# A diffusion transformer block on eight cores: FFN weight loads wait for their own prepared tile instead of for all of them

## The reference

```python
mod = (_silu(L0_c) @ L0_wmod).reshape(8, 6, 1, -1)     # sa, ca, ga, sb, cb, gb
h = _layernorm(x) * (1 + ca) + sa
x = x + ga * local_attn(h, Wq, Wk, Wv, Wo)             # 16 heads, window 512
h = _layernorm(x) * (1 + cb) + sb
gate = silu((h @ fp8(gate_w)) * gate_scale)            # 2048 -> 6144
up   = (h @ fp8(up_w)) * up_scale                      # 2048 -> 6144
x = x + gb * ((gate * up) @ fp8(down_w)) * down_scale  # 6144 -> 2048
```

## Time and profile before

| | us |
|---|---|
| time, median of 2 runs | 4372.17 (4331.66 and 4412.68) |
| the profiled execution, its own time | 4323.63 |
| its span (slowest core, core 4) | 4322.1 |
| TensorE matmuls busy | 3254.9 (75%) |
| VectorE / ScalarE / GpSimd busy | 795.2 / 773.0 / 387.8 |

### The profile page before, as it was taken

One profiled execution on the slowest core, in us unless ns is written; L12 is line 12 of the kernel. 1 busy time (PEld: TensorE's weight loads), 2 busy tenths in 40 slices (PEclk: granted clock), 3 DMA queues, 4 the chain that ended last, 5 costly groups with the idle time before them and its releaser, 6 DMA issues.

```text
span 4322.1 us, 48357 instructions; the slowest of 8 cores (4306.8 to 4322.1 us)
## 1 busy us (share of the span) xinstructions
PE 3254.9 (75%) x16778; PEld 1534.0 (35%) x16778; DVE 795.2 (18%) x1682; ACT 773.0 (18%) x1329; POOL 387.8 (9%) x520
## 2 busy tenths in 40 slices
PE   2344559976666699400299996999969999789999
PEld 0011224444443444200144443444434444344444
DVE  3200100035555510200011013111130110311101
ACT  2100401146565522200001002100011100021100
POOL 1001000011212111222100000000100000000000
PEclk9566679998889899655699997999979999889999
DMA  8897462477777778877522232222422223312233
GB/s 175 172 152 125 70 67 25 39 69 63 61 63 61 63 80 98 102 62 61 73 77 78 88 120 95 78 74 86 124 103 69 78 74 117 130 56 78 75 113 100
DMA packets 475303, 377.73 MB, mean 87 GB/s; under 512 B 384928, under 2 KB 387680, under 8 KB 470720
## 3 DMA queue, kind: packets, MB, share of 16 engines
q0 software_dynamic: 372928, 181.67, 35.5%
q1 hardware_dynamic: 102144, 192.97, 13.9%
HBM read 505.40 MB, written 62.96 MB: 132 GB/s over the span
## 4 chain that ended last, share of the span: by engine, by line
PE 55%; DMA 30%; issue 7%; DVE 3%; another core or an unknown queue 2%; ACT 1%; POOL 0%; DVEq 0%; POOLq 0%; ACTq 0%; SPq 0%
PE PSf L857 16%; PE PSf L919 15%; PE PSf L867 15%; DMA u_scr<-pre 8%; DMA g_scr<-pre 8%; DMA d_scr<-pre 7%; DMA wmodb<-wmod 5%; PE PSf L544 4%; DMA s_x<-x 2%; PE PSf L500 1%; PE PSf L517 1%; DVE sumx L788 1%; PE PSf L381 1%; ACT h L445 1%
## 5 line engine op out<-in xcount | busy, mean ns | idle before, releaser
L857 PE MATMUL PSf<-h,g 128*128 128x512 bf16 x3072 | 703.7, 383 | 315.9 <-DMA g<-g_scr 312.5
L867 PE MATMUL PSf<-h,u8w 128*128 128x512 bf16 x3072 | 694.4, 379 | 0.0
L919 PE MATMUL PSf<-fuse,d 128*128 128x512 bf16 x3072 | 676.2, 380 | 8.0 <-DVE fuse L884 8.0
L857 PEld LDWEIGHTS PSf<-h,g 128*128 128x128 fp8e4 x3072 | 302.6, 99 | 685.4 <-issue 329.4
L884 DVE SCALAR_TENSOR_TENSOR fuse<-PSf,gsus,sy 128x512 bf16<-128x512 f32 x192 | 144.2, 751 | 1565.8 <-ACT sy L879 1565.8
L867 PEld LDWEIGHTS PSf<-h,u8w 128*128 128x128 fp8e4 x3072 | 300.6, 98 | 362.5
L919 PEld LDWEIGHTS PSf<-fuse,d 128*128 128x128 fp8e4 x3072 | 298.8, 98 | 360.7 <-issue 14.4
L879 ACT ACTIVATE sy<-PSf,gsus 128x512 bf16<-128x512 f32 x192 | 131.9, 687 | 1164.3 <-PE PSf L867 1164.2
L381 PE MATMUL PSf<-wmodb,csi 128*1 128x512 bf16 x384 | 154.9, 566 | 227.1 <-DMA wmodb<-wmod 212.6
L580 PE MATMUL PSf<-k_fm,q_fm 128*128 128x512 bf16 x256 | 112.8, 441 | 214.5 <-ACT s_p L645 209.0
L620 DVE TENSOR_REDUCE negmax<-PSf 128x1 f32<-128x640 f32 x256 | 209.4, 818 | 222.9 <-PE PSf L586 222.1
(11 more groups left out here) (105 smaller groups left out, 2135.6 us busy)
## 6 DMA issues: line engine op xcount, KB each, us to landing
wmodb<-wmod POOLq DMA_DIRECT2D x64, 768.0 KB, 15.8
g<-g_scr SPq DMA_DIRECT2D x192, 256.0 KB, 2.6
u8w<-u_scr SPq DMA_DIRECT2D x192, 256.0 KB, 2.9
d<-d_scr SPq DMA_DIRECT2D x64, 768.0 KB, 4.6
s_x<-x SPq DMA_DIRECT2D x16, 1024.0 KB, 12.8
s_u<-x SPq DMA_DIRECT2D x16, 1024.0 KB, 7.1
s_xe<-x POOLq DMA_DIRECT2D x64, 256.0 KB, 4.2
y<-x3p POOLq DMA_DIRECT2D x64, 256.0 KB, 4.3
```

The lines of the kernel that those rows point to most:

```text
L857: ev("pe", lambda e, par=par, kc=kc: e.matmul(bankf(0 + par), g8[:, par, :].rearrange("p (c n) -> p c n", c=16)[:, kc, :].bitcast(F8), h2[ ...
L867: ev("pe", lambda e, par=par, kc=kc: e.matmul(bankf(2 + par), u8w[:, par, :].rearrange("p (c n) -> p c n", c=16)[:, kc, :].bitcast(F8), h2 ...
L919: ev("pe", lambda e, par=par, m=m_, dbk=dbk: e.matmul(bankf(dbk), d8[:, par, :].rearrange("p (a n) -> p a n", a=NM)[:, m, :].bitcast(F8), ...
```

## The change

The preparation steps of gate and up are put in turn (gate 0, up 0, gate 1, ...), and the FFN's loads wait for the store of the tile that they read. `st_done` holds for each step the counter and the value that its store raises it to; `pre_st` is a copy. Gate tile m is now step 2m, up tile m step 2m + 1, down tile dc the steps 96 + 3 dc to 96 + 3 dc + 2.

```diff
     for m in range(NM):
         pre_steps.append((gw[:, m * 128:(m + 1) * 128].rearrange(
             "(c p) n -> p c n", p=128), g_scr[m]))
-    for m in range(NM):
         pre_steps.append((uw[:, m * 128:(m + 1) * 128].rearrange(
             "(c p) n -> p c n", p=128), u_scr[m]))
...
     PRE_A, PRE_B = dScr2[0].n, dScr2[1].n
+    pre_st = dict(st_done)
...
-            w0 = [(dScr2[0], PRE_A), (dScr2[1], PRE_B)]
+            w0 = [pre_st[2 * m]]
...
             ev("sy", lambda e, m=m, par=par: e.dma_start(u8w[:, par, :],
                                                          u_scr[m]),
-               sc=dU[par])
+               sc=dU[par], waits=[pre_st[2 * m + 1]])
...
-            w0 = []
+            w0 = [pre_st[96 + 3 * dc + 1], pre_st[96 + 3 * dc + 2]]
             if Q == 0 and dc < 2:
-                w0 = [(c_av, 256), (c_pt, 256), (c_qk, 256),
-                      (dScr2[0], PRE_A), (dScr2[1], PRE_B)]
+                w0 += [(c_av, 256), (c_pt, 256), (c_qk, 256)]
             elif dc < 2:
-                w0 = [(c_fpe, dn_prev[14 + dc])]
+                w0 += [(c_fpe, dn_prev[14 + dc])]
             else:
-                w0 = [(c_fpe, dn_mm_done[dc - 2])]
+                w0 += [(c_fpe, dn_mm_done[dc - 2])]
```

## The result

| | before | changed |
|---|---|---|
| median us | 4332.26 (10 runs, from 4318.45) | 4028.09 (11 runs, from 4023.08) |
| profiled execution: time / slowest span | 4323.63 / 4322.1 | 4023.81 / 4022.3 |

The ratio of the changed kernel to the kernel before is 0.9312, with a 95% interval of 0.9282 to 0.9343: faster by 6.9%.

The account below looks back on a forecast made before the run. Bound: TensorE idle 312.5 us (core 4) before the gate matmuls, g waiting for all 144 preparation steps. Core 1's 4319.5 − 303.3 = 4016.2, plus 1.5 outside the span, other terms 0: 4018 us (4005 to 4030; overall range 4000 to 4100).

Parts of the forecast that it names:

- the gap: Before the first quarter's gate matmuls: TensorE's 312.5 us wait for g on core 4 falls to about 0.3 us.
- The order of the steps at nothing: Gate and up preparation in turn: worth 0, as all 96 steps end near 1729, before h at 1818.
- the 89 us of margin: Time from gate and up weights being in memory, near 1729, to h being ready at 1818.
- The steps beside gate and up: 37 preparation steps beside first gate and up: 9.57 us each (ends 8.36 and 12.3), last store issued at 2169.
- the rule of turns packet by packet: DMA engines alternate between queues by packet; worked out as g landing in 3.0 us and steps at 12.3 us.
- The g and u loads at nothing: Gate and up loads under the steps: price 0; upper end 3.9 us a pair, about 195 us in all.
- The d loads: First down stage: loads wait only for their own three steps, and no stall comes, even at 12.3 us a step.
- The epilogue behind the preparation: Rival, chance 0.20: s_xe loads late behind GpSimd's steps, price 0 to 73 us; halfway a 36 us stall, 4054 us.
- The deadline of 43.6 us after the start of down: GpSimd must be free by then: transposition dc = 4 at 63.05 us, less 2.5 for adds and 17 for s_xe loads.
- The sum: Each core's span less its gap plus 0.3; core 1 slowest at 4016.2, plus 1.5 outside the span: 4018 us.

Follow-up runs that it names:

- The two runs on the order: Changed kernel with the old step order: 4021 to 4028 us, ratio 0.9272; kernel before with only the new order: ratio 0.9991.
- the one on the d waits: Changed kernel, first two down-weight loads of the first quarter again waiting for all 144 steps: 4050.3 and 4046.2 us.
- The late runs: 56 more preparation steps ahead of the 144, in the changed kernel and in it with the old order: 4505.9 and 4505.8 us.
- the run without the steps: Changed kernel without the 48 down-weight preparation steps, d loads reading prepared gate tiles instead: 4014.4 and 4014.3 us, ratio 0.9247.

## Why the prediction was right, and where it was not

**What bounds the kernel, and the gap.** Right. The two runs on the order and the one on the d waits leave the waits of g and u as the owner of the 312 us but for some 20. The start of the gate matmuls was forecast for 1818 and is 1807.7 to 1819.0 by core.

**The order of the steps at nothing.** Right. I had tied it to the 89 us of margin. The late runs suggest that it holds somewhat beyond: down starts within 5 us in the mean in either order, because gate and up cannot end before step 96 and a pair is shorter than a step. They are single executions, and their total time cannot tell.

**The steps beside gate and up.** 9.57 us a step was forecast from the output projection, 9.43 measured; the last store at 2169, found at 2153.9 to 2172.7 by core. Displaced were 0.30 of the added points, not 0.40. The total of 92% says that there was more room in the engines than the 86% of the output projection suggested. I had worked out two numbers from the rule of turns packet by packet (the Trainium skill, DMA: Bandwidth & Descriptors, "Queues, rings and completion order"), and the trace bears out neither: g landed in 4.6 us where I made it 3.0, and the steps took 9.43 us where I made it 12.3. That speaks against my working and not surely against the rule: the page's packet is a group of typically 9 to 17 descriptors, and I had counted every row of 2 KB as a packet.

**The g and u loads at nothing.** The mechanism was right, the size was off by a little: the term was 0 and the stage became 4.0 us longer in the mean (1.9 to 7.2 us by core over the 335.9 of the run without the steps). I had compared the median landing, 6.2 us for the larger tiles, with the 6.9 us of a pair, and priced the slower loads only as an end that I did not take. The median of g did stay below (4.6 us), but single loads took up to 8.6 us, and each core waited for one to three of them. On core 6 the last pair came on top: SyncE issues both first d loads (1.5 MB) right behind it, the last up tile landed in 12.6 us and came 2.4 us late, and the wait cost more than its length, since TensorE went on at a granted clock of 0.68.

**The d loads.** Right: none was waited for in the changed kernel, and the 21 to 25 us of the run that undoes their waits are the value of that part of the change, which I had folded into the gap.

**The epilogue behind the preparation.** The rival with 0.20. On the chip of the result it did not come (26 to 45 us in hand where 28 were forecast). On two others it did without any step added, with up to 8.6 us in the changed kernel and 14.6 in the run with the second d load late. The deadline of 43.6 us after the start of down was right within 4.5 us in every core that waited for the first epilogue behind it. What was missing is the second deadline behind it, that of the y stores, which only shows once the first is taken away.

**The sum.** 4018 forecast, 4024 in the profiled execution, 4028 in the median. By core it was not right: I took core 1 for the slowest because its gap was the shortest, and it is the fastest, 3999.1 us, since h is ready there at 1808 where 1819 stood before. Which core is late changes from execution to execution, so a span less its own gap does not name the slowest. Worked out for all eight cores it gives 4006.5 us in the mean, and 4012.4 was measured: 5.9 us more, 4.3 of them the longer gate and up stage. That the forecast of the time is only 6 us off is thus in part luck: the core was the wrong one, and the growth of the stage was priced at nothing.

## What to carry to other kernels

A wait for the end of a queue of transfers can be made to cost nothing by waiting for the one that is read; before that, look how far the needed part has come at the time of the wait (here 89 us ahead), since it tells whether the wait can go altogether and whether a new order of the queue is worth anything. Then go through everything that stands behind the long queue on its issuing engine: once the wait is gone, the queue's tail runs beside new work, and its neighbours in the same order get a deadline. Work it out for each of them (last issue, what follows, who needs it when), and for the next one behind it too. And where loads run beside the tail, compare their slowest landing, not the median, with the time that they have.

## What the runs showed that I had not expected

- With the steps beside it a 256 KB g tile landed in 4.6 us (median) in place of 2.6, and two 768 KB d tiles issued together behind the last pair in up to 13.5 us in place of a median of 4.6; GpSimd waited 13.17 us there for a store that takes 7. Since each load has a whole pair's time, TensorE lost only some 4 us of it.
- The same program prepares its weights at a different speed on another chip: the last store at 2154 to 2173 us on one, at 2195 to 2227 us on another, where the kernel before took 4368 us in place of 4332. Why the second is slower was not tried. It is enough to use up the 26 to 45 us of margin.
- Two lists of loads in a different order, with 25 waits of up to 5.8 us or 40 of up to 4.1 us on core 0, cost TensorE nearly the same, 93.0 and 96.1 us up to the down stage.
